# Masked attention layer with residual and norm on one core: 2304 instead of 2048 columns turned by DMA, adjacency loads split over two queues

## The chip, the cores and the metric

The kernel runs on one core of one Trainium2 chip. Its time is device time in microseconds (us). The engines of the core work side by side, each through its own list of instructions in order: TensorE (PE, with weight loads shown apart as PEld), VectorE (DVE), ScalarE (ACT), GpSimd (POOL) and SyncE (SP), which here only issues DMAs. They wait for each other by semaphores.

## The reference

```
q = x @ Wq.T + bq ; k = x @ Wk.T + bk ; v = x @ Wv.T + bv      # x is 4096 x 128, float32
scores = q @ k.T / sqrt(128)                                    # 4096 x 4096
scores = where(adj > 0, scores, -9e15)                          # adj is 4096 x 4096 int32
att = softmax(scores, axis=-1) @ v
out = layernorm(x + elu(att), axis=-1)                          # 4096 x 128
```

## The kernel before

The 4096 rows are cut in 32 tiles of 128 rows. q and k are kept in SBUF as two float16 parts each (high and low), so that three float16 matmuls give the scores of a block, and the probabilities too are split in a high and a low part before they are multiplied with v. Before the loop the projections are made; after it the last tile is finished by code of its own.

The main loop is written out as periods. Period p has eight steps j = 0 to 7 on PE, ACT and DVE, and works on several tiles at once:

- PE, in each step: the scores of 512 columns of tile p (`scores`, three matmuls); then, in the steps that `T_AT` names, the transposes of one group of 512 columns of tile p-1 or p-2 (`transposes`, four 128x128 blocks into `ps_t`); then the products with v of one group of tile p-2 in the order of `PV_ORDER` (`values`, eight matmuls).
- DVE: after every second step it adds the mask to 1024 columns of scores and takes the maximum (`masked_piece`, L589), and then turns 1024 columns of adjacency into a mask (`mask_piece`, L575). In between it makes the low parts of transposed groups (`low_part`, L604).
- ACT: the exponential of 1024 columns (`exp_piece`, L453), the high parts of transposed groups (`high_part`, L462), the high parts of rows that a DMA will turn (`high_rows`, L470), and parts of the ELU and the norm of tile p-3 (`attention` L476, `elu_exp`, `row_sum` L488, `square_sum` L492).
- POOL: the low parts of the rows that a DMA will turn (`low_rows`, L322, in pieces of 256 columns), between the small operations of ELU and norm of tile p-3 (L329 to L364).
- SP: the DMAs. `turn` transposes `p_rows[c]` (high and low halves side by side) into `p_turned[c]`; `load_half` brings half a tile of adjacency (1 MB); `store` writes a tile of output.

So a probability column reaches the product with v in one of two ways. Columns 2048 to 4095 (groups 4 to 7) are transposed on PE, copied by ACT and completed by DVE. Columns 0 to 2047 (c = 0 and c = 1) are split by ACT and POOL and transposed by DMA. The numbers at the top of the file set this:

```
DMA_COLS = (PIECE, PIECE)                  # 1024 and 1024 columns
T_AT = {4: 6, 5: 7, 6: 8, 7: 10}           # step of the transposes; 8 and 10 are 0 and 2 of the next period
PV_ORDER = (4, 5, 6, 0, 1, 7, 2, 3)        # group whose values PE takes in step 0, 1, ..., 7
```

ACT takes the high part of a group one step label after its transposes, DVE its low part likewise. The mask of a piece of scores is made three pieces ahead of its use. SP issues in a period: the turn of c = 1, the second half of the adjacency of tile p+1, the store, the turn of c = 0, and the first half of the adjacency of tile p+2.

Of the kernel before, what the change touches and what calls it, by code (L numbers as in the profile page):

```python
# [13 lines left out]
P = 128  # L14
# [15 lines left out]
LOW_PARTS = 4  # L30
# [6 lines left out]
def attention_kernel(nc, x, adj, wq, bq, wk, bk, wv, bv, out):  # L37
# [8 lines left out]
    with ExitStack() as ctx:  # L46
# [155 lines left out]
        def pv_count(i, g):  # L202

            return STEPS * i + PV_ORDER.index(g) + 1

        def exp_count(i, c):

            return PIECES * i + c + 1

# [25 lines left out]
        def _(sp):  # L235
# [44 lines left out]
            period(0, 0, head=False, turns_0=False, turns_1=False, stores=False)  # L280
# [6 lines left out]
            period(TILES - 2, 0, loads=False)  # L287
            period(TILES - 1, 1, head=False, loads=False)
# [12 lines left out]
        def _(pool):  # L301
# [14 lines left out]
            def low_rows(i, s, c):  # L316

                pool.wait_ge(rows_hi, BY_DMA * i + c + 1)
                w = DMA_COLS[c]
                for b in range(LOW_PARTS):  # L320
                    cols = slice(b * w // LOW_PARTS, (b + 1) * w // LOW_PARTS)
# [82 lines left out]
        def _(act):  # L404
# [51 lines left out]
            def high_part(i, s, g, first):  # L456
# [15 lines left out]
            def attention(i, s):  # L472

                act.wait_ge(recip_ready, i + 1)
                act.wait_ge(pv_done, STEPS * (i + 1))
# [19 lines left out]
            def last_high_part(g):  # L495

                act.wait_ge(last_pt, g - LAST_PE + 1)
                act.wait_ge(pv_done, STEPS * LAST)
                nc.scalar.activation(last_high(g), last_ps[g], ACT.Copy).then_inc(last_hi_act, 1)

            def period(p, n, has_1=True, has_2=True, has_3=True, warm=True):

                for j in range(STEPS):
                    if not warm:
# [24 lines left out]
            period(0, 0, has_1=False, has_2=False, has_3=False, warm=False)  # L529
# [3 lines left out]
            with act.Fori(2, TILES // 2) as pair:  # L533
                for n in range(2):
                    period(2 * pair + n, n)
            high_part(LAST - 1, 0, 5, False)
# [21 lines left out]
        def _(dve):  # L558
# [19 lines left out]
            def masked_piece(i, s, c, first):  # L578

                cols = slice(c * PIECE, (c + 1) * PIECE)  # L580
                if not first:
                    if c < BY_DMA:
                        dve.wait_ge(rows_lo, BY_DMA * (i - 2) + c + 1)
# [17 lines left out]
            def low_part(i, s, g):  # L601
                k = g - FIRST_PE
                dve.wait_ge(phi_ready, PE_GROUPS * i + k + 1)
                nc.vector.tensor_tensor(p_lo[:, k, :], ps_t[bank_of(s, g)][:, :], p_hi[:, k, :],  # L604
# [8 lines left out]
            def late_high_part(g):  # L613
# [3 lines left out]
                dve.wait_ge(pv_done, STEPS * (LAST - 1))  # L617
                nc.vector.tensor_copy(p_hi[:, k, :], ps_t[bank_of(0, g)][:, :]).then_inc(phi_ready, 1)

            def last_high_part(g):  # L620

                dve.wait_ge(last_pt, g - LAST_PE + 1)
                dve.wait_ge(pv_done, STEPS * (LAST - 1))
# [41 lines left out]
            def period(p, n, has_scores=True, has_1=True, has_2=True, warm=True, makes_mask=True):  # L665

                for j in range(STEPS):
# [14 lines left out]
                    if j == 1 and has_scores:  # L682
                        mask_piece(p, n, 3)
                    if j in (3, 5, 7) and has_scores and makes_mask:
                        mask_piece(p + 1, 1 - n, j // 2 - 1)


            for n in range(AHEAD):
                low_of_projection(n)
                if n > AHEAD - PIECES:  # L690
                    mask_piece(0, 0, n - AHEAD + PIECES - 1)
# [7 lines left out]
            low_part(LAST - 1, 0, 5)  # L699
# [13 lines left out]
        def _(pe):  # L713
# [70 lines left out]
            def transposes(i, s, g, first):  # L784
# [7 lines left out]
                for b in range(BLOCKS):  # L792
# [4 lines left out]
            def values(i, s, g, first):  # L797

                if g >= FIRST_PE:
                    pe.wait_ge(plo_ready, PE_GROUPS * i + g - FIRST_PE + 1)  # L800
                elif g % 2 == 0 or pv_count(0, g - 1) > pv_count(0, g):
                    pe.wait_ge(turned[g // 2], 16 * i + 16)
                if g == PV_ORDER[0] and not first:
# [5 lines left out]
                for b in range(BLOCKS):  # L809
                    k = g * BLOCKS + b  # L810
                    if g >= FIRST_PE:
                        high = p_hi[:, g - FIRST_PE, b * P:(b + 1) * P]
                        low = p_lo[:, g - FIRST_PE, b * P:(b + 1) * P]
                    else:
                        high = p_turned[g // 2][s][:, g % 2 * BLOCKS + b, :]
                        low = p_turned[g // 2][s][:, DMA_COLS[g // 2] // P + g % 2 * BLOCKS + b, :]
                    nc.tensor.matmul(ps_out[s][:, 0:2 * D], high, v_parts[:, k, :],  # L817
                                     start=(g == PV_ORDER[0] and b == 0), stop=False)
                    last = nc.tensor.matmul(ps_out[s][:, D:2 * D], low, v_parts[:, k, D:2 * D],  # L819
                                            start=False, stop=(g == PV_ORDER[-1] and b == BLOCKS - 1))  # L820
# [27 lines left out]
            def period(p, n, has_scores=True, has_1=True, has_2=True, warm=True, first=False):  # L848

                for j in range(STEPS):  # L850
# [12 lines left out]
                    if has_2:  # L863
                        values(p - 2, n, PV_ORDER[j], first)

# [11 lines left out]
            values(LAST - 1, 0, 4, False)  # L877
            values(LAST - 1, 0, 0, False)
            values(LAST - 1, 0, 1, False)
            transposes(LAST - 1, 0, 7, False)  # L880
            values(LAST - 1, 0, 5, False)
# [3 lines left out]
            for g in (7, 2, 3):  # L885
                values(LAST - 1, 0, g, False)
# [25 lines left out]
```

## Time and profile before

| | us |
|---|---|
| median of 3 runs (lowest, highest) | 434.79 (434.63, 434.86) |
| the profiled execution's own time | 434.68 |
| its span, first to last instruction | 432.8 |

| engine | busy us (share of the span) |
|---|---|
| PE | 422.2 (98%) |
| DVE | 364.2 (84%) |
| ACT | 355.2 (82%) |
| POOL | 344.5 (80%) |

The mean granted clock of TensorE is 0.996 of full speed. The queue q1, which carries all the large DMAs, has packets in flight for 92.5% of 16 engines' span; this sum counts overlapping packets twice, since it passes 1.00 in some stretches, so it is no measure of how full the DMA engines are. Ends of matmuls are modelled; their starts are what spacing is read from.

### The profile page before, as it was taken

Reading aid. Unit: us, or ns where it says so; the run is one execution under the profiler, and the core shown is the slowest. Engines: PE = TensorE matmul, PEld = TensorE weight load, DVE = VectorE, ACT = ScalarE, POOL = GpSimd, SP = SyncE. Lnnn points to the kernel's source line nnn. Section 1 sums busy time; section 2 is a strip of 40 time slices with the busy share of each in tenths; the row PEclk is TensorE's granted clock in tenths of the full one; section 3 lists DMA queues with packets and bytes.
Section 4 is the critical chain, followed back from the end, with each engine's and each line's share of the span. In section 5 each row is a group of like instructions: output and inputs, shape, how many; then the busy total and the mean of one; then the engine's idle time right before and its main releaser. Section 6 shows DMA issues by size and latency. Waiting matters only on the chain.

```text
span 432.8 us, 11401 instructions
## 1 busy us (share of the span) xinstructions
PE 422.2 (98%) x3479; PEld 310.9 (72%) x3479; DVE 364.2 (84%) x671; ACT 355.2 (82%) x737; POOL 344.5 (80%) x613
## 2 busy tenths in 40 slices
PE   8998899999999999999999999999999999999994
PEld 6564677777777777777777777777777777777783
DVE  1787998888889898888889988888898988888784
ACT  4779778888888888888888988888888988888892
POOL 0065558889888988898888988898889888898874
PEclk9999999999999999999999999999999999999998
DMA  8934999999999999999999999999999999999551
GB/s 225 380 111 121 259 271 229 258 230 267 285 268 264 266 258 278 256 271 254 261 266 270 252 254 281 272 256 245 271 266 267 251 263 274 264 252 239 103 87 36
DMA packets 149932, 104.76 MB, mean 242 GB/s; under 512 B 133024, under 2 KB 141728, under 8 KB 141728
## 3 DMA queue, kind: packets, MB, share of 16 engines
q1 hardware_dynamic: 149488, 104.41, 92.5%
q10 hardware_dynamic: 432, 0.20, 0.2%
q8 instruction: 6, 0.10, 0.1%
q14 instruction: 6, 0.05, 0.0%
HBM read 69.47 MB, written 2.10 MB: 165 GB/s over the span
## 4 chain that ended last, share of the span: by engine, by line
POOL 58%; issue 18%; PE 16%; ACT 3%; DVE 3%; POOLq 2%; ACTq 0%; DVEq 0%
POOL p_rows L322 25%; POOL res L336 6%; POOL rstd L360 4%; POOL neg_mean L347 3%; POOL y L341 3%; POOL var L356 3%; POOL att_sum L329 3%; POOL att L331 3%; PE ps_out L817 3%; POOL centred L349 2%; POOL expm L338 2%; POOL var_eps L358 2%; PE ps_scores L778 2%; PE ps_scores L779 2%; POOL y_out L364 2%
## 5 line engine op out<-in xcount | busy, mean ns | idle before, releaser
L322 POOL TENSOR_TENSOR p_rows<-scores,p_rows 128x256 f16<-128x256 f32 x252 | 176.0, 728 | 8.6 <-ACT p_rows L470 8.6
L589 DVE CUSTOM_DVE_ANT_0 scores<-ps_scores,adj 128x1024 f32<-128x1024 f32 x128 | 156.1, 1219 | 14.8 <-issue 11.3
L453 ACT ACTIVATE scores<-scores,neg_max 128x1024 f32<-128x1024 f32 x128 | 145.7, 1138 | 0.7 <-DVE neg_max L598 0.5
L575 DVE TENSOR_SCALAR adj<-adj 128x1024 f32<-128x1024 int32 x128 | 105.1, 821 | 0.0
L604 DVE TENSOR_TENSOR p_lo<-ps_t,p_hi 128x512 f16<-128x512 f32 x124 | 82.6, 685 | 26.1 <-ACT p_hi L462 25.9
L778 PE MATMUL ps_scores<-k_hi,q_hi 128*128 128x512 f16 x256 | 97.0, 379 | 0.1
L779 PE MATMUL ps_scores<-k_lo,q_hi 128*128 128x512 f16 x256 | 97.0, 379 | 0.0
L780 PE MATMUL ps_scores<-k_hi,q_lo 128*128 128x512 f16 x256 | 97.0, 379 | 0.0
L817 PE MATMUL ps_out<-v_parts,p_hi 128*128 128x256 f16 x496 | 95.3, 273 | 0.7 <-DVE p_lo L604 0.7
L817 PE MATMUL ps_out<-v_parts,p_turned 128*128 128x256 f16 x496 | 95.0, 273 | 0.0
L819 PE MATMUL ps_out<-v_parts,p_lo 128*128 128x128 f16 x496 | 88.5, 219 | 0.0
L819 PE MATMUL ps_out<-v_parts,p_turned 128*128 128x128 f16 x496 | 88.4, 219 | 0.0
L462 ACT ACTIVATE p_hi<-ps_t 128x512 f16<-128x512 f32 x122 | 71.7, 587 | 19.2 <-PE ps_t L794 18.1
L794 PEld LDWEIGHTS ps_t<-ident,scores 128*128 128x128 f32 x496 | 61.6, 141 | 25.8 <-ACT scores L453 2.6
L794 PE MATMUL ps_t<-ident,scores 128*128 128x128 f32 x496 | 74.5, 273 | 1.6 <-ACT scores L453 1.1
L470 ACT ACTIVATE p_rows<-scores 128x1024 f16<-128x1024 f32 x63 | 66.0, 1047 | 0.0
L817 PEld LDWEIGHTS ps_out<-v_parts,p_hi 128*128 128x128 f16 x496 | 48.5, 98 | 18.4 <-DVE p_lo L604 10.5
L817 PEld LDWEIGHTS ps_out<-v_parts,p_turned 128*128 128x128 f16 x496 | 48.5, 98 | 11.3
L819 PEld LDWEIGHTS ps_out<-v_parts,p_turned 128*128 128x128 f16 x496 | 48.5, 98 | 7.8
L819 PEld LDWEIGHTS ps_out<-v_parts,p_lo 128*128 128x128 f16 x496 | 48.5, 98 | 4.4
L780 PEld LDWEIGHTS ps_scores<-k_hi,q_lo 128*128 (+1 forms) x256 | 25.1, 98 | 30.2
L488 ACT ACTIVATE act_junk<-y 128x128 f32<-128x128 f32 x31 | 9.6, 310 | 37.0 <-POOL y L341 37.0
(92 smaller groups left out, 475.9 us busy)
## 6 DMA issues: line engine op xcount, KB each, us to landing
adj<-in_adj_dram SPq DMA_DIRECT2D x64, 1024.0 KB, 5.5
out_dram<-y_out SPq DMA_DIRECT2D x32, 64.0 KB, 5.1
x_rows<-in_x_dram SPq DMA_DIRECT2D x4, 256.0 KB, 4.4
x_rows<-in_x_dram SPq DMA_DIRECT2D x2, 512.0 KB, 6.6
p_turned<-p_rows SPq DMA_TRANSPOSE x63, 4.7
w_rows<-in_L_gnn_Wq_dram ACTq DMA_DIRECT2D x1, 64.0 KB, 2.7
w_rows<-in_L_gnn_Wk_dram ACTq DMA_DIRECT2D x1, 64.0 KB, 3.3
w_rows<-in_L_gnn_Wv_dram ACTq DMA_DIRECT2D x1, 64.0 KB, 3.9
```

The lines of the kernel that those rows point to most:

```text
L322: last = nc.gpsimd.tensor_tensor(p_rows[c][:, w:][:, cols], s_sb[s][:, c * PIECE:c * PIECE + w][:, cols], p_rows[c][:, 0:w][:, cols], ALU. ...
L453: nc.scalar.activation(s_sb[s][:, cols], s_sb[s][:, cols], ACT.Exp, bias=neg_max[:, s:s + 1], accum_out=p_sums[:, s, c:c + 1]).then_inc(ex ...
L462: nc.scalar.activation(p_hi[:, k, :], ps_t[bank_of(s, g)][:, :], ACT.Copy).then_inc(phi_ready, 1)
L575: nc.vector.tensor_scalar(mask_sb[s][:, cols], adj_sb[s][:, cols], 0.0, MASKED / SCALE, ALU.is_le, ALU.mult).then_inc(mask_ready, 1)
L589: nc.vector.tensor_tensor_reduce(out=s_sb[s][:, cols], in0=ps_scores[c % 2][:, :], in1=mask_sb[s][:, cols], scale=SCALE, scalar=-3.0e38, o ...
L604: nc.vector.tensor_tensor(p_lo[:, k, :], ps_t[bank_of(s, g)][:, :], p_hi[:, k, :], ALU.subtract).then_inc(plo_ready, 1)
L778: nc.tensor.matmul(place, q_hi[:, rows], k_hi[:, cols], start=True, stop=False)
L779: nc.tensor.matmul(place, q_hi[:, rows], k_lo[:, cols], start=False, stop=False)
L780: last = nc.tensor.matmul(place, q_lo[:, rows], k_hi[:, cols], start=False, stop=True)
L794: last = nc.tensor.transpose(ps_t[bank][:, b * P:(b + 1) * P], s_sb[s][:, kb * P:(kb + 1) * P], ident[:, :])
L817: nc.tensor.matmul(ps_out[s][:, 0:2 * D], high, v_parts[:, k, :], start=(g == PV_ORDER[0] and b == 0), stop=False)
L819: last = nc.tensor.matmul(ps_out[s][:, D:2 * D], low, v_parts[:, k, D:2 * D], start=False, stop=(g == PV_ORDER[-1] and b == BLOCKS - 1))
```

## The change

Columns 2048 to 2303, the first half of group 4, go the DMA's way: `p_rows[1]` and `p_turned[1]` grow from 1024 to 1280 columns. PE transposes only the two other blocks of group 4, in the same step as group 5, and group 7 one step earlier. The order of the values becomes 5, 4 (two blocks), 6, then 7 and 0 in one step, 1, 2, 3, and last the two turned blocks of group 4. Masks are made one piece ahead of their use. The first half of the adjacency of tile p+1 is issued by ACT in step 3 of period p; the second half stays on SP, behind the turn of c = 1.

```diff
-DMA_COLS = (PIECE, PIECE)
+MIXED_COLS = 256
+DMA_COLS = (PIECE, PIECE + MIXED_COLS)
+MIXED = FIRST_PE
-T_AT = {4: 6, 5: 7, 6: 8, 7: 10}
-PV_ORDER = (4, 5, 6, 0, 1, 7, 2, 3)
+T_AT = {4: 6, 5: 6, 6: 8, 7: 9}
+PV_STEPS = ((5,), (4,), (6,), (7, 0), (1,), (2,), (3,), (TURNED_HALF,))
-LOW_PARTS = 4
+LOW_COLS = 256
...
+        def by_pe(g):
+            return slice(MIXED_COLS, BANK) if g == MIXED else slice(0, BANK)
...
-            def period(p, n, head=True, turns_0=True, turns_1=True, stores=True, loads=True):
+            def period(p, n, turns_0=True, turns_1=True, stores=True, loads=True):
                 if turns_1:
                     turn(p - 2, n, 1)
-                if head:
+                if loads:
                     load_half(p + 1, 1 - n, 1, False)
                 if stores:
                     store(p - 4, n)
                 if turns_0:
                     turn(p - 1, 1 - n, 0)
-                if loads:
-                    load_half(p + 2, n, 0, False)
...
             def low_rows(i, s, c):
-                for b in range(LOW_PARTS):
+                for b in range(w // LOW_COLS):
...
             def high_part(i, s, g, first):
-                nc.scalar.activation(p_hi[:, k, :], ps_t[bank_of(s, g)][:, :], ACT.Copy).then_inc(phi_ready, 1)
+                nc.scalar.activation(p_hi[:, k, by_pe(g)], ps_t[bank_of(s, g)][:, by_pe(g)], ACT.Copy).then_inc(phi_ready, 1)
             def high_rows(i, s, c, first):
-                act.wait_ge(exp_done, exp_count(i, c))
+                act.wait_ge(exp_done, exp_count(i, (c * PIECE + w - 1) // PIECE))
...
+            def load_first_half(i, slot):
+                act.wait_ge(masked_ready, PIECES * (i - 2) + 2)
+                cols = slice(0, 2 * PIECE)
+                act.dma_start(adj_sb[slot][:, cols], adj_tiled[i, :, cols]).then_inc(adj_in[slot][0], 16)
+
                 for j in range(STEPS):
+                    if j == 3 and loads:
+                        load_first_half(p + 1, 1 - n)
...
-                    if j == 1 and has_scores:
-                        mask_piece(p, n, 3)
-                    if j in (3, 5, 7) and has_scores and makes_mask:
-                        mask_piece(p + 1, 1 - n, j // 2 - 1)
+                    if j in (1, 3, 5) and has_scores:
+                        mask_piece(p, n, j // 2 + 1)
+                    if j == 7 and has_scores and makes_mask:
+                        mask_piece(p + 1, 1 - n, 0)
```

On PE, in steps 1 to 3 of a period of the loop, the order before is as follows (`p_turned_0` is a buffer of `p_turned[0]`; matmuls of the same kind follow each other where a pair is shown).

```order
L778 MATMUL ps_scores<-k_hi,q_hi 128x512
L779 MATMUL ps_scores<-k_lo,q_hi 128x512
L780 MATMUL ps_scores<-k_hi,q_lo 128x512
L794 MATMUL ps_t<-ident,scores 128x128 x4
L800 REGISTER_ALU
L817 MATMUL ps_out<-v_parts,p_hi 128x256
L819 MATMUL ps_out<-v_parts,p_lo 128x128
```

These are the rows of step 2: scores, the transposes of group 7, the values of group 6. The changed kernel has in steps 1 and 3:

```order
L808 MATMUL ps_t<-ident,scores 128x128 x4
L836 MATMUL ps_out<-v_parts,p_hi 128x256
L838 MATMUL ps_out<-v_parts,p_lo 128x128
L836 MATMUL ps_out<-v_parts,p_hi 128x256
L838 MATMUL ps_out<-v_parts,p_lo 128x128
L792 MATMUL ps_scores<-k_hi,q_hi 128x512
```
```order
L836 MATMUL ps_out<-v_parts,p_hi 128x256
L838 MATMUL ps_out<-v_parts,p_lo 128x128
L819 ISA
L836 MATMUL ps_out<-v_parts,p_turned_0 128x256
L838 MATMUL ps_out<-v_parts,p_turned_0 128x128
```

The first piece is step 1: the transposes of group 7 now stand there, before two blocks of values of group 4. The second is step 3: the last values from `p_hi` and `p_lo` (group 7) stand ahead of the first turned ones (group 0); before, group 7 stood two steps later.

On DVE, from the start of a period, before:

```order
L604 TENSOR_TENSOR p_lo<-ps_t,p_hi 128x512
L603 REGISTER_ALU
L604 TENSOR_TENSOR p_lo<-ps_t,p_hi 128x512
L583 ISA
L586 ISA
L589 ISA scores,max_parts<-ps_scores,adj 128x1024
L589 ISA max_parts 128x1
L608 ISA
L609 TENSOR_REDUCE p_sum<-p_sums 128x1
L611 RECIPROCAL recip<-p_sum 128x1
L574 ISA
L575 TENSOR_SCALAR adj<-adj 128x1024
```

and after:

```order
L619 TENSOR_TENSOR p_lo<-ps_t,p_hi 128x512
L598 ISA
L601 ISA
L604 ISA scores,max_parts<-ps_scores,adj 128x1024
L604 ISA max_parts 128x1
L623 ISA
L624 TENSOR_REDUCE p_sum<-p_sums 128x1
L626 RECIPROCAL recip<-p_sum 128x1
L589 ISA
L590 TENSOR_SCALAR adj<-adj 128x1024
L618 REGISTER_ALU
L619 TENSOR_TENSOR p_lo<-ps_t,p_hi 128x512
```

One of the two low parts at the head has gone to the period before. The low part of group 7 stands, before and after, behind the first masked piece, the reciprocal and the mask.

On ACT, from the copy of the attention output to the next exponential, before:

```order
L476 ACTIVATE att<-ps_out,recip 128x256
L467 ISA
L469 REGISTER_ALU
L470 ACTIVATE p_rows<-scores 128x1024
L459 REGISTER_ALU
L461 REGISTER_ALU
L462 ACTIVATE p_hi<-ps_t 128x512
L453 ACTIVATE scores,p_sums<-scores,neg_max 128x1024
```

and after:

```order
L482 ACTIVATE att<-ps_out,recip 128x256
L465 REGISTER_ALU
L467 REGISTER_ALU
L468 ACTIVATE p_hi<-ps_t 128x512
L473 ISA
L475 REGISTER_ALU
L476 ACTIVATE p_rows<-scores 128x1024
L509 REGISTER_ALU
L511 ISA
L511 DMA adj<-in_adj_dram 128x2048
L459 ACTIVATE scores,p_sums<-scores,neg_max 128x1024
```

The high part of group 7 has moved ahead of the rows for the DMA, and the load stands behind them.

## Rows read from the trace of the kernel before

**Rows 1.** Stretch: us; busy PE, PEld, DVE, ACT, POOL; PEclk, DMA share, GB/s.
```profile
200.00:250.00 50.00, 50.00 (x428) 37.08 (x427) 44.08 (x81) 41.70 (x88) 43.94 (x79) 1.00 0.99 264
```
**Rows 2.** Timeline of PE: start us, us, instruction, count.
```profile
204.06 0.38 PE L778 MATMUL ps_scores<-k_hi,q_hi 128*128 128x512 f16 x1
...
204.71 0.60 PE L794 MATMUL ps_t<-ident,scores 128*128 128x128 f32 x4
...
205.15 0.27 PE L817 MATMUL ps_out<-v_parts,p_hi 128*128 128x256 f16 x1
...
205.81 0.38 PE L778 MATMUL ps_scores<-k_hi,q_hi 128*128 128x512 f16 x1
...
206.24 0.38 PE L780 MATMUL ps_scores<-k_hi,q_lo 128*128 128x512 f16 x1
...
208.90 0.38 PE L778 MATMUL ps_scores<-k_hi,q_hi 128*128 128x512 f16 x1
...
209.55 0.27 PE L817 MATMUL ps_out<-v_parts,p_turned 128*128 128x256 f16 x1
```
**Rows 3.** Timeline of DVE, same stretch.
```profile
205.76 1.27 DVE L604 TENSOR_TENSOR p_lo<-ps_t,p_hi 128x512 f16<-128x512 f32 x2
206.95 1.21 DVE L589 CUSTOM_DVE_ANT_0 scores<-ps_scores,adj 128x1024 f32<-128x1024 f32 x1
...
208.35 0.78 DVE L575 TENSOR_SCALAR adj<-adj 128x1024 f32<-128x1024 int32 x1
209.15 0.69 DVE L604 TENSOR_TENSOR p_lo<-ps_t,p_hi 128x512 f16<-128x512 f32 x1
...
211.04 1.06 DVE L575 TENSOR_SCALAR adj<-adj 128x1024 f32<-128x1024 int32 x1
```
**Rows 4.** Timeline of POOL over one period.
```profile
202.57 2.57 POOL L322 TENSOR_TENSOR p_rows<-scores,p_rows 128x256 f16<-128x256 f32 x4
...
208.54 3.01 POOL L322 TENSOR_TENSOR p_rows<-scores,p_rows 128x256 f16<-128x256 f32 x4
211.52 0.90 POOL L336 TENSOR_TENSOR res<-pos,x_rows 128x128 f32<-128x128 f32 x1
...
214.82 2.57 POOL L322 TENSOR_TENSOR p_rows<-scores,p_rows 128x256 f16<-128x256 f32 x4
```
**Rows 5.** What POOL's L329 waited for, 100 to 390 us: us, times.
```profile
  ACT att L476: 9.5, 23
```
**Rows 6.** Timeline of ACT.
```profile
201.13 0.31 ACT L488 ACTIVATE act_junk<-y 128x128 f32<-128x128 f32 x1 [1.26 <-POOL y L341]
...
201.44 1.04 ACT L470 ACTIVATE p_rows<-scores 128x1024 f16<-128x1024 f32 x1
```
**Rows 7.** POOL in the last periods, where DVE makes no masks.
```profile
407.17 0.45 POOL L336 TENSOR_TENSOR res<-pos,x_rows 128x128 f32<-128x128 f32 x1
...
415.58 2.56 POOL L322 TENSOR_TENSOR p_rows<-scores,p_rows 128x256 f16<-128x256 f32 x4
```
**Rows 8.** Timeline of SP's DMA issues.
```profile
70.69 2.76 SPq L263 DMA_TRANSPOSE p_turned<-p_rows  x1
...
205.24 3.00 SPq L263 DMA_TRANSPOSE p_turned<-p_rows  x1
208.48 0.39 SPq L249 DMA_DIRECT2D adj<-in_adj_dram  x1
...
388.66 3.12 SPq L263 DMA_TRANSPOSE p_turned<-p_rows  x1
```
**Rows 9.** DMA by issue: KB each, median us from issue to landing.
```profile
adj<-in_adj_dram SPq DMA_DIRECT2D x64, 1024.0 KB, 5.5
...
p_turned<-p_rows SPq DMA_TRANSPOSE x63, 4.7
```
**Rows 10.** Stretches with loads alone (first) and a turn alone, columns as rows 1.
```profile
14.00:19.00 5.00, 5.00 (x21) 2.29 (x20) 3.84 (x6) 3.65 (x7) 0.00 (x0) 1.00 1.01 426
...
421.50:422.50 1.00, 1.00 (x15) 0.93 (x13) 0.75 (x2) 1.00 (x5) 0.84 (x4) 1.00 1.27 290
```

More of the change, by code:

```diff
@@ L286, in _ @@
                     period(2 * pair + n, n)
-            period(TILES - 2, 0, loads=False)
-            period(TILES - 1, 1, head=False, loads=False)
+            period(TILES - 2, 0)
+            period(TILES - 1, 1, loads=False)
             turn(LAST - 1, 0, 1)
@@ L527, in period @@
                         square_sum(p - 3, 1 - n, pool_done, POOL_OPS * (p - 3))
-            period(0, 0, has_1=False, has_2=False, has_3=False, warm=False)
+            period(0, 0, has_1=False, has_2=False, has_3=False, warm=False, loads=False)
             period(1, 1, has_2=False, has_3=False, warm=False)
@@ L532, in _ @@
             period(3, 1)
-            with act.Fori(2, TILES // 2) as pair:
+            with act.Fori(2, TILES // 2 - 1) as pair:
                 for n in range(2):
                     period(2 * pair + n, n)
-            high_part(LAST - 1, 0, 5, False)
+            period(LAST - 1, 0)
+            period(LAST, 1, loads=False)
             exp_piece(LAST, 1, 0, False)
@@ L581, in masked_piece @@
                 if not first:
[L582 to L583 removed]
+                    if 2 * c <= MIXED:
+                        dve.wait_ge(rows_lo, BY_DMA * (i - 2) + min(c + 1, BY_DMA))
                     if 2 * c + 1 >= FIRST_PE:
@@ L791, in transposes @@
                     pe.wait_ge(plo_ready, PE_GROUPS * i + k - 1)
-                for b in range(BLOCKS):
+                for b in range(by_pe(g).start // P, BLOCKS):
                     kb = g * BLOCKS + b
@@ L795, in transposes, with values @@
                 last.then_inc(pt_ready, 1)
-            def values(i, s, g, first):
-                if g >= FIRST_PE:
+            def values(i, s, part, first):
+                g = MIXED if part == TURNED_HALF else part
+                by_dma = part < FIRST_PE or part == TURNED_HALF
+                c = min(g // 2, BY_DMA - 1)
+                if not by_dma:
                     pe.wait_ge(plo_ready, PE_GROUPS * i + g - FIRST_PE + 1)
-                elif g % 2 == 0 or pv_count(0, g - 1) > pv_count(0, g):
-                    pe.wait_ge(turned[g // 2], 16 * i + 16)
-                if g == PV_ORDER[0] and not first:
+                elif part % 2 == 0:
+                    pe.wait_ge(turned[c], 16 * i + 16)
+                if part == PV_ORDER[0] and not first:
                     pe.wait_ge(att_ready, i - 1)
@@ L862, in period @@
                             transposes(p - 1, 1 - n, g, not warm)
-                    if has_2:
-                        values(p - 2, n, PV_ORDER[j], first)
+                    for g in PV_STEPS[j]:
+                        if has_2:
+                            values(p - 2, n, g, first)
             period(0, 0, has_1=False, has_2=False, warm=False)
@@ L876, in _ @@
             transposes(LAST - 1, 0, 6, False)
-            values(LAST - 1, 0, 4, False)
-            values(LAST - 1, 0, 0, False)
-            values(LAST - 1, 0, 1, False)
+            for part in (5, 4, 0, 1):
+                values(LAST - 1, 0, part, False)
             transposes(LAST - 1, 0, 7, False)
-            values(LAST - 1, 0, 5, False)
             values(LAST - 1, 0, 6, False)
@@ L884, in _ @@
             last_transposes(3)
-            for g in (7, 2, 3):
-                values(LAST - 1, 0, g, False)
+            for part in (7, 2, 3, TURNED_HALF):
+                values(LAST - 1, 0, part, False)
             for g in range(FIRST_PE, STEPS):
```

41 lines of the change are left out of this document (22 added, 19 removed).

## The prediction

> **What bounds the kernel now.** I read the table of stretches first. In the middle of the run PE is busy for 50.00 us of 50, at full clock, while POOL has 43.94, DVE 44.08 and ACT 41.70 [rows 1]. So PE sets the pace of the loop, and the reader should ask at once how far behind it the others are. The pace itself: the turn of c = 1 is issued at 70.69, 205.24 and 388.66 us, which is 12.23 us per tile over 26 periods [rows 8]. With the two or three periods on either side of these I count 29 that run at this pace.
>
> Then the timelines, engine by engine over one period. On PE a step takes 0.65 us for its scores (208.90 to 209.55), 0.44 for four transposes (204.71 to 205.15) and 0.66 for eight matmuls of values (205.15 to 205.81) [rows 2]. Eight steps and four sets of transposes make 8 x 1.31 + 4 x 0.44 = 12.24, so PE has next to no waits in its 12.23.
>
> POOL comes second, and closer than its 88% says. Its waits are mostly answers that it has to wait for whatever the pace. The one that shows slack is L329's wait for ACT's copy of the attention output, 9.5 us in 23 periods, 0.41 us each [rows 5]. If PE went faster or POOL had more to do, that 0.41 is what it could give.
>
> The DMA side looks full at 0.99 [rows 1], but it is not. Loads alone move 426 GB/s, a turn alone 290, and the share reads 1.27 there [rows 10]. Two loads of 1.05 MB at 426 are 4.9 us and two turns of 0.52 MB at 290 are 3.6 us, together 8.5 of 12.23.
>
> **The change, part by part.**
>
> PE's work. Per tile two transposes of 128 columns go: 2 x 0.11 = 0.22 us. Number and kind of the scores and values stay. PE alone would then need 12.23 - 0.22 = 12.01 us per tile. Over 29 periods this is the gain on offer, 6.4 us.
>
> PE's new wait, the first term that decides. The values of group 7 move from step 5 to step 3. They need DVE's low part of group 7, and DVE makes that behind the first masked piece, the reciprocal and a mask, before as after. I count from the start of step 0, at 204.06. PE now begins step 1 at 1.75, as before; step 2 at 1.75 + 0.65 + 0.44 + 0.33 (half a set of values) = 3.17; step 3 at 3.17 + 0.65 + 0.66 = 4.48; it wants the values of group 7 at 4.48 + 0.65 = 5.13 [rows 2]. DVE starts the first masked piece at 206.95, which is 2.89, the mask at 4.29, the low part at 5.09, and ends it at 209.84, which is 5.78 [rows 3]. DVE was busy with two low parts until 207.03, of which one is now earlier; but the masked piece also needs the third scores matmul of step 1, which starts at 206.24 and lasts 0.38 [rows 2], so it can come forward by at most about 0.15 us. The low part ends at 5.63 to 5.78, and PE waits 0.50 to 0.65 us. Behind it stand the values of group 0, the scores of step 4 and all else on PE; nothing on PE makes the time up. PE's loop becomes 12.01 + 0.58 = 12.59 us.
>
> POOL's work, the second term. `low_rows` of c = 1 gets a fifth piece: 2.57 / 4 = 0.64 us, or 3.01 / 4 = 0.75 where DVE's masks lie across it [rows 4]. ACT's `high_rows` of c = 1 grows from 1024 to 1280 columns, 1.04 x 256 / 1024 = 0.26 us by proportion. This lies on POOL's path too: POOL makes y, ACT sums it (start 201.13), makes the high rows (201.44 to 202.48), and POOL starts the low rows at 202.57 [rows 4, 6]. Against these stands the 0.41 of slack. POOL's loop is 12.23 - 0.41 + 0.64 + 0.26 = 12.72 us. What is uncertain is how DVE's masks lie on POOL. `res` takes 0.90 us and four low pieces 3.01 with masks, 0.45 and 2.56 at the end, where DVE makes none [rows 4, 7]: a mask costs POOL up to 0.45 us when POOL has work under it. If one of the four masks falls in an idle stretch, the loop is 12.27; with the dearer piece and no relief it is 12.83.
>
> On this point the Trainium skill (SBUF — State Buffer, section "SBUF: two separate sides") says that VectorE in a two-port mode and GpSimd share one pair of ports under an exclusive lock, and that the one that starts first keeps it for the whole instruction. The doubled `res` agrees, and so does the mask of 1.06 us at 211.04, beside 0.78 at 208.35 [rows 3]. By that rule a POOL piece begun just before the mask of step 1 would hold that mask too; this is the third rival below.
>
> The other edits, at nothing. The high part of group 4 shrinks by half, and that of group 7 moves ahead of the high rows of c = 0 on ACT; ACT has idle time of 1.26 us per tile in front of L488, where it waits for POOL's y [rows 6], and this hides the 0.39 us too that the load's issue would cost it if it costs ACT what it costs SP [rows 8]. If that cover went, it would be 0.39 per tile at most. The masks keep their number and their places in DVE's list; only which piece is made changes. The turn of c = 1 has 2560 packets' worth instead of 2048: its 3.00 us of issue become about 3.75 and its landing goes from 4.7 to about 5.5 [rows 8, 9]; its first reader is PE in step 5 and ACT's next high rows, 8 us after the issue. Below nothing, the changed order could save a little in the first tiles, since two masks are no longer made ahead of the loop; I give it nothing.
>
> The load of the first half is issued by ACT behind the high rows of c = 0, at about 209, and needed by the mask of step 7, which stood at 205.12 + 12.23 = 217.35 in this frame. It lands 5.5 us after its issue if alone [rows 9], at 214.5. But SP issues the second half at the same time (208.48, plus 0.75 for the longer turn) [rows 8]. Both at 426 GB/s need 4.9 us instead of 2.5, so it lands at about 217. That is just in time, and I count nothing.
>
> **The sum.** The loop takes the slower of PE's 12.59 and POOL's 12.72. The new idle of POOL in front of the low rows gives a mask a place to fall for free, so I take a little off the second: 12.65 us. That is 0.42 more than 12.23, times 29 = 12.2 us. The profiled execution took 434.68 us (its span 432.8 and 1.9 around it); 434.68 + 12.2 = 446.9. The median of the runs lies 0.11 above the profiled one, so I predict 447.0 us. Its own range is 441 to 453, a loop of 12.45 to 12.85.
>
> **The rivals.**
>
> A. PE goes on setting the pace, faster than before. The point that decides is when DVE ends the low part of group 7: at 5.13 us PE waits for nothing, the loop is 12.01 and the time 434.8 - 6.4 = 428.4. To break even it must come at 5.35, 0.3 or more ahead of my 5.63. POOL must also keep within 12.23, which asks that more than one mask stops holding it. For this speaks that the trace shows one phase only between DVE and POOL, and four masks could cost POOL little in another; against it, that DVE's chain from the scores of step 1 is made of durations alone, without a wait in it. Chance 0.06.
>
> B. The two loops come out near the old one: one mask free of POOL (12.27), and a wait on PE of 0.2 to 0.3. Then the time is 434 to 436. Chance 0.03.
>
> C. The mask of step 1 is held by a POOL piece: 1.06 instead of 0.78, 0.28 more on PE's wait, a loop of 12.9. That is 29 x 0.67 = 19.4 more, 454. For it speaks that POOL will now be late against PE, so that its pieces lie elsewhere; against it, that in the trace small operations of 0.46 us stand there. Chance 0.09.
>
> D. The first half of the adjacency comes late. Each 0.5 us that the mask of step 7 waits for beyond its time delays the masked piece of the next step 1, and with it the low part of group 7: 12.65 + 0.5, which is 29 x 0.92 = 27 more, 461. For it speaks that two loads and soon a turn share the engines; against it, that a longer period also moves the mask of step 7 later by 0.4. Chance 0.10.
>
> E. My forecast, 0.72.
>
> About 0.2% is what a measurement of this kernel can tell from no change. Faster: 0.06, same: 0.03, slower: 0.91. The range for 8 in 10 goes from 438, a loop of 12.34, near POOL's lower bound, to 457, which takes in C and the mild half of D.
>
> **What would show it.** In the profile after: PE's busy time below its span in the loop, with its longest wait in front of the values of `p_hi` for DVE's p_lo, near 0.6 us per tile, in step 3. POOL's wait of L329 for ACT gone to nearly nothing, and a new one in front of its fifth-piece group for ACT's p_rows. Five low pieces in the second group. ACT's wait for y longer than 1.26. The turn of c = 1 spaced at 12.65. No wait of DVE for adj; were there one, D holds. My forecast is wrong if the turns come at 12.23 or less, or if PE shows no wait in step 3.

## The result, and the profile after

| | before | after |
|---|---|---|
| median (lowest, highest), us | 434.82 (434.63, 434.86) | 462.37 (458.29, 464.78) |
| ratio, 95% interval | | 1.0624 [1.0583, 1.0665] |
| profiled execution: time; span | 434.68; 432.8 | 464.78; 463.0 |
| first copy of the attention output starts | 60.24 | 67.58 |
| spacing of these copies, mean over 24 periods (4th to 28th) | 12.228 | 12.986 |
| from the 28th copy to the end of the span | 42.4 | 45.0 |

The changed kernel is 6.2% slower, where 447.0 with a range to 457 was forecast: the direction holds, the time lies outside the range. Ratios are of fast runs alone, within 1.5% of the fastest of the same kernel, which leaves out two of e4's four. The profiled execution is the slowest of the four; the sums below are made against its own span. The 30.2 us of it come from three places: 7.3 before the first copy, 20.2 in the 27 periods up to the 28th, and 2.7 at the end. The forecast had only the second, at 12.2.

The page, engines first, then the stretch that answers to [rows 1]:

```profile
PE 423.7 (92%) x3417; PEld 301.3 (65%) x3417; DVE 349.7 (76%) x671; ACT 358.6 (77%) x737; POOL 346.0 (75%) x644
```
```profile
200.00:250.00 50.00, 47.37 (x397) 34.19 (x398) 39.56 (x76) 40.30 (x87) 41.98 (x79) 1.00 0.93 260
```

PE, busy without a gap before, now has 2.6 us of idle in 50, at full clock, and no engine took its place: every one is less busy than before. A loop of waits sets the pace. The spacing itself, by ACT's copies:

```profile
197.53 0.46 ACT L482 ACTIVATE att<-ps_out,recip 128x256 f32<-128x256 f32 x1
...
210.16 0.46 ACT L482 ACTIVATE att<-ps_out,recip 128x256 f32<-128x256 f32 x1
...
223.36 0.46 ACT L482 ACTIVATE att<-ps_out,recip 128x256 f32<-128x256 f32 x1
...
235.99 0.47 ACT L482 ACTIVATE att<-ps_out,recip 128x256 f32<-128x256 f32 x1
```

12.63, 13.20, 12.63: the short periods have the length forecast (12.65), and every second one is longer, mostly by 0.5 to 0.75. PE's timeline of the long one shows two waits (for [rows 2]; before, the first row of values stood 0.22 after the start of the third scores matmul):

```profile
212.05 0.38 PE L794 MATMUL ps_scores<-k_hi,q_lo 128*128 128x512 f16 x1
212.90 0.28 PE L836 MATMUL ps_out<-v_parts,p_hi 128*128 128x256 f16 x1 [0.47 <-DVE p_lo L619]
...
215.97 0.38 PE L794 MATMUL ps_scores<-k_hi,q_lo 128*128 128x512 f16 x1
216.76 0.28 PE L836 MATMUL ps_out<-v_parts,p_turned 128*128 128x256 f16 x1 [0.41 <-DMA p_turned<-p_rows]
```

The first is step 3 and group 7: 212.90 - 212.05 - 0.22 = 0.63 us, the wait that was forecast. The second is step 5 and group 2, the first reader of the turn of c = 1: 0.57 us, and it was forecast to be free. What PE's weight loads waited for, in total (us, times, longest), over the whole span; the matmuls behind them waited 15.5 and 13.0 us, and of the second sum one wait of 5.7 is that of the start:

```profile
PEld ps_out L836 <- DVE p_lo L619: 30.5, 31, 1.7
...
PEld ps_out L836 <- DMA p_turned<-p_rows: 20.7, 16, 6.2
```

The turn that PE waits for there, on SP and in the DMA, with the load that ACT issues beside it (for [rows 8, 9]):

```profile
208.87 3.04 SPq L272 DMA_TRANSPOSE p_turned<-p_rows  x1
```
```profile
210.67 0.34 ACTq L511 DMA_DIRECT2D adj<-in_adj_dram  x1
```
```profile
L272 SPq DMA_TRANSPOSE p_turned<-p_rows x1: 3041/3041/3041, 208.9 to 208.9; - x1
...
DMA to landing us min/median/max: 7.8/7.8/7.8
```

208.87 + 7.8 is 216.67, and PE starts at 216.76. In the short period that follows, the turn is issued at 221.51 and lands in 7.5, and its first reader starts at 229.39, 7.9 behind the issue, without a wait. The turn of c = 0 one half period before the late one, with no load of ACT's near its issue, lands in 5.9. Over the turns issued between 80 and 390 us, those of c = 1 land in 7.7 (median; 6.4 to 8.1) and those of c = 0 in 6.4 (5.9 to 7.4); before it was 4.7 and 4.6.

The late landing has a mark of its own. SP ends the issue of the turn of c = 1 after 3.0 us, as quickly as before, and the landing comes 4.6 us behind that end (median; 3.4 to 5.0). For the turns of c = 0 it comes 2.0 behind it, and before the change 1.7 for both.

POOL, for [rows 4] (c = 1 first, then c = 0 and `res`), and ACT's wait for y, for [rows 6]:

```profile
205.49 3.28 POOL L328 TENSOR_TENSOR p_rows<-scores,p_rows 128x256 f16<-128x256 f32 x5 [0.49 <-ACT p_rows L476]
...
212.13 3.01 POOL L328 TENSOR_TENSOR p_rows<-scores,p_rows 128x256 f16<-128x256 f32 x4 [0.43 <-ACT p_rows L476]
215.10 0.45 POOL L342 TENSOR_TENSOR res<-pos,x_rows 128x128 f32<-128x128 f32 x1
```
```profile
216.47 0.31 ACT L494 ACTIVATE act_junk<-y 128x128 f32<-128x128 f32 x1 [1.42 <-POOL y L347]
```

The fifth piece costs 3.28 - 2.57 = 0.71. `res` takes 0.45 instead of 0.90: one of DVE's masks no longer lies across it, as the forecast had allowed for.

The late start is one event. ACT and POOL, whose first high and low rows of 1280 columns wait:

```profile
59.64 1.27 ACT L476 ACTIVATE p_rows<-scores 128x1280 f16<-128x1280 f32 x1 [8.89 <-DMA p_turned<-p_rows]
```
```profile
60.99 3.18 POOL L328 TENSOR_TENSOR p_rows<-scores,p_rows 128x256 f16<-128x256 f32 x5 [9.41 <-ACT p_rows L476]
```

They wait for a turn that SP issued at 46.25; ACT issued its first load 0.8 us behind it, SP the second half at 48.67, and the turn landed after 13.3 us:

```profile
46.25 2.37 SPq L272 DMA_TRANSPOSE p_turned<-p_rows  x1
48.67 1.08 SPq L258 DMA_DIRECT2D adj<-in_adj_dram  x1
```
```profile
47.04 0.33 ACTq L511 DMA_DIRECT2D adj<-in_adj_dram  x1
```
```profile
L272 SPq DMA_TRANSPOSE p_turned<-p_rows x1: 2369/2369/2369, 46.2 to 46.2; - x1
...
DMA to landing us min/median/max: 13.3/13.3/13.3
```

The next turn, of c = 0, starts its issue at 51.67, and that takes 10.2 us. Meanwhile the engines are idle and the DMA's share is as high as ever, while it moves a fraction of the 290 to 426 GB/s of [rows 10]:

```profile
55.00:56.00 1.00, 0.00 (x0) 0.00 (x0) 0.90 (x3) 0.00 (x0) 0.00 (x0) 1.00 1.35 84
56.00:57.00 1.00, 0.00 (x0) 0.00 (x0) 0.00 (x0) 0.00 (x0) 0.00 (x0) 1.00 1.30 57
57.00:58.00 1.00, 0.00 (x0) 0.00 (x0) 0.00 (x0) 0.00 (x0) 0.00 (x0) 1.00 1.21 36
```

### The profile page after: what moved, and what is told of

It is laid out like the page before. It is cut to its first block, busy times and chain, and to the rows that moved or that the text cites. A ratio compares the mean times of both kernels' runs of the same rounds, so it can differ in the third digit from the quotient of the medians.

```text
span 463.0 us, 11266 instructions
## 1 busy us (share of the span) xinstructions
PE 423.7 (92%) x3417; PEld 301.3 (65%) x3417; DVE 349.7 (76%) x671; ACT 358.6 (77%) x737; POOL 346.0 (75%) x644
## 4 chain that ended last, share of the span: by engine, by line
POOL 52%; DMA 13%; ACT 11%; issue 11%; PE 11%; POOLq 1%; DVE 1%; ACTq 0%; SPq 0%; DVEq 0%
POOL p_rows L328 32%; DMA p_turned<-p_rows 12%; ACT p_rows L476 8%; POOL rstd L366 4%; POOL y L347 3%; POOL att L337 2%; POOL res L342 2%; POOL att_sum L335 2%; PE ps_t L732 2%; POOL expm L344 2%; PE ps_out L743 2%; POOL var L362 1%; POOL y_out L370 1%; POOL var_eps L364 1%; ACT act_junk L494 1%
## 5 line engine op out<-in xcount | busy, mean ns | idle before, releaser
L328 POOL TENSOR_TENSOR p_rows<-scores,p_rows 128x256 f16<-128x256 f32 x283 | 198.2, 731 | 43.4 <-ACT p_rows L476 43.4
L836 PE MATMUL ps_out<-v_parts,p_turned 128*128 128x256 f16 x558 | 109.2, 274 | 13.0 <-DMA p_turned<-p_rows 13.0
L838 PE MATMUL ps_out<-v_parts,p_turned 128*128 128x128 f16 x558 | 100.8, 220 | 0.0
L836 PE MATMUL ps_out<-v_parts,p_hi 128*128 128x256 f16 x434 | 85.2, 273 | 15.5 <-DVE p_lo L619 15.5
L619 DVE TENSOR_TENSOR p_lo<-ps_t,p_hi 128x256 f16<-128x256 f32 (+1 forms) x124 | 76.6, 619 | 24.7 <-ACT p_hi L468 23.9
L468 ACT ACTIVATE p_hi<-ps_t 128x256 f16<-128x256 f32 (+1 forms) x122 | 66.0, 542 | 29.5 <-PE ps_t L808 27.9
L476 ACT ACTIVATE p_rows<-scores 128x1024 f16<-128x1024 f32 (+1 forms) x63 | 73.1, 1160 | 9.9 <-DMA p_turned<-p_rows 9.5
L838 PE MATMUL ps_out<-v_parts,p_lo 128*128 128x128 f16 x434 | 78.3, 219 | 0.0
L836 PEld LDWEIGHTS ps_out<-v_parts,p_turned 128*128 128x128 f16 x558 | 54.7, 98 | 34.6 <-DMA p_turned<-p_rows 20.7
L836 PEld LDWEIGHTS ps_out<-v_parts,p_hi 128*128 128x128 f16 x434 | 42.4, 98 | 37.5 <-DVE p_lo L619 30.5
L808 PE MATMUL ps_t<-ident,scores 128*128 128x128 f32 x434 | 63.0, 274 | 2.3 <-ACT scores L459 2.3
L838 PEld LDWEIGHTS ps_out<-v_parts,p_turned 128*128 128x128 f16 x558 | 54.8, 98 | 9.1
```

The lines of the kernel that those rows point to most:

```text
L476: nc.scalar.activation(p_rows[c][:, 0:w], s_sb[s][:, c * PIECE:c * PIECE + w], ACT.Copy).then_inc(rows_hi, 1)
L619: nc.vector.tensor_tensor(p_lo[:, k, by_pe(g)], ps_t[bank_of(s, g)][:, by_pe(g)], p_hi[:, k, by_pe(g)], ALU.subtract).then_inc(plo_ready, 1)
L808: last = nc.tensor.transpose(ps_t[bank][:, b * P:(b + 1) * P], s_sb[s][:, kb * P:(kb + 1) * P], ident[:, :])
```

## The experiments

Each ran beside the kernel before on the same chip. "After" in a kernel's description is the changed kernel. "Spacing" is the mean of the 24 periods as in the table above, "start" the first copy of the attention output; before has 12.228 and 60.24.

| kernel | median us (range) | ratio [95%] | spacing | start |
|---|---|---|---|---|
| e1 columns part alone | 447.14 (446.97–447.82) | 1.0278 [1.0260, 1.0295] | 12.618 | 60.44 |
| e2 loads and masks part alone | 434.89 (434.52–435.61) | 0.9998 [0.9988, 1.0007] | 12.238 | 59.95 |
| e3 after, POOL four pieces | 448.34 | 1.0298 [1.0281, 1.0315] | 12.628 | 61.41 |
| e4 after, group 7 in step 5 | 462.9, of 461.04 and 464.81; of all four 466.91 (461.04–469.48) | 1.0635 [1.0584, 1.0686] | 13.082 | 66.86 |
| e5 e1, group 7 in step 5 | 446.36 (445.27–447.32) | 1.0257 [1.0239, 1.0276] | 12.603 | 59.47 |
| e6 e5, POOL four pieces | 440.98 (438.34–443.72) | 1.0150 [1.0092, 1.0208] | 12.377 | 59.40 |
| e7 after, ACT's load in step 5 | 450.56 (448.19–453.15) | 1.0344 [1.0305, 1.0384] | 12.620 | 66.54 |
| e9 e5, fifth piece on DVE | 441.50 (440.42–443.67) | 1.0146 [1.0126, 1.0166] | 12.366 | 59.37 |
| e12 e1, old order | 445.41 (445.18–445.81) | 1.0243 [1.0226, 1.0260] | 12.585 | 59.79 |
| e10 e12, fifth piece on DVE | 443.88 (442.33–444.30) | 1.0209 [1.0192, 1.0226] | 12.497 | 60.31 |
| e11 after, first three loads on SP | 457.42 (456.96–457.90) | 1.0514 [1.0496, 1.0531] | 13.011 | 59.95 |
| e13 e12 with 128 columns | 435.87 (435.20–437.19) | 1.0027 [1.0015, 1.0038] | 12.260 | 60.19 |

**The two halves of the change.** e1 keeps the 2304 columns and the new order, with loads and masks as before:

```diff
+                if loads:
+                    load_half(p + 2, n, 0, False)
...
-                    if j == 3 and loads:
-                        load_first_half(p + 1, 1 - n)
...
-                    if j in (1, 3, 5) and has_scores:
-                        mask_piece(p, n, j // 2 + 1)
+                    if j == 1 and has_scores:
+                        mask_piece(p, n, 3)
...
```

> The 2304 columns, the new order of transposes and values, but both loads on SP's queue at their old places and the masks three pieces ahead as before. Theory 1 (the loop is set by POOL and ACT, and the load on ACT's queue costs about 8 us once in the first tiles plus some turns that come late): the 8 us go and the loop loses its long odd periods, about 13.0 to 12.65 us per tile, so 443 to 448 us. Rival 1 (the longer turn itself is what comes late, whichever queue the loads are on): no more than 3 us below the changed kernel, 457 to 462. Rival 2 (PE's wait for the low part of group 7 sets the loop): 12.5 us per tile and 442 us.

e2 is the reverse, the kernel before with ACT's load and the later masks:

```diff
...
+                    if j == 3 and loads:
+                        load_first_half(p + 1, 1 - n)
...
```

> The kernel before, with 2048 columns by DMA and its own order on PE, but the loads split over the two queues and the masks one piece ahead as in the changed kernel. Theory 1: the first tiles cost about 8 us more, and in the loop PE still sets the pace at 12.23 us, so 441 to 444 us. Rival 1 (only the longer turn is at fault): 435 us, no change. A third view (a load beside a turn delays every turn enough to stall PE in every period): over 450 us.

e1 takes 447.14, the forecast time, and its start is on time. e2 takes nothing. So the columns cost 12.4 us, the loads by themselves 0, and together there are 15 more: an interaction. In e1 SP queues the second half of the adjacency right behind the longer turn, and in the middle of the run the turn lands in 5.3:

```profile
L272 SPq DMA_TRANSPOSE p_turned<-p_rows x1: 3570/3570/3570, 204.9 to 204.9; - x1
...
DMA to landing us min/median/max: 5.3/5.3/5.3
```

Over all turns of c = 1 from 80 to 390 us the median in e1 is 5.0. But the range goes from 4.8 to 7.3: in e1's first periods SP issues each turn about 1 us behind a load, and the issue itself is held up.

```profile
96.63 0.35 SPq L258 DMA_DIRECT2D adj<-in_adj_dram  x1
97.47 5.16 SPq L272 DMA_TRANSPOSE p_turned<-p_rows  x1
```

This turn lands in 7.2, still only 2.0 us behind the end of its issue. So one queue alone can make a turn late too, by a load ahead of it. What one queue never shows in the loop of e1 is a quick issue and a late landing: there the landing comes 1.5 us behind the end of the issue in the median and 2.1 at most, in the changed kernel 4.6.

In e2 ACT's load is issued at 207.38, when SP has just ended the issue of the turn of c = 1 (205.12 to 207.05), and the turn lands in 4.4. The turns of c = 0 land in 5.9 there, where they landed in 4.6 before, and nobody waits for them.

**The two terms of the sum.** e3 drops POOL's fifth piece from the changed kernel; the low parts of columns 2048 to 2303 are zeros, set once. e4 puts group 7 in step 5.

```diff
-                for b in range(w // LOW_COLS):
+                for b in range(min(4, w // LOW_COLS)):
```

> The changed kernel without POOL's fifth piece: the low parts of columns 2048 to 2303 are left out (that part of p_rows holds zeros, set once before the loop), all else the same. Theory 1 (POOL's loop): 0.64 us less per tile on POOL, so the loop falls until PE with its wait for group 7 takes over at about 12.5: 13.0 to 12.5, some 14 us below the changed kernel, 446 to 450 us. Rival 2 (PE's wait sets the loop): no change, 458 to 465. Rival 3 (late turns set it): no change either.

```diff
-PV_STEPS = ((5,), (4,), (6,), (7, 0), (1,), (2,), (3,), (TURNED_HALF,))
+PV_STEPS = ((5,), (4,), (6,), (0,), (1,), (7, 2), (3,), (TURNED_HALF,))
```

> The changed kernel with the values of group 7 taken in step 5 as before the change, ahead of those of group 2, instead of in step 3. Theory 1: PE's wait of about 0.45 us in step 3 goes, but POOL's loop stays, so no more than 3 us less, 458 to 463 us. Rival 2 (PE's wait for group 7 sets the loop): 0.45 x 29 = 13 us less, about 449 us.

e3 saves 14 us. Its turns of c = 1 land as late as ever (median 7.5), but POOL's work was on their path: they are now issued earlier relative to PE, and the weight loads wait for `p_turned` 1.1 us in four times between 100 and 390 us. What stays is PE's loop alone, 12.628. e4 saves nothing: PE, without its wait in step 3, runs into the turned columns, for which its weight loads wait 35.3 us in 20 times over the span (its profile, and with it its spacing, is of an execution of 469.01 us). With that in the way e4 says nothing of PE's term, so e5 repeats e4's diff on e1, where from 100 to 390 us no matmul waits for a turn, and e6 repeats e3's diff on top of e5.

> The columns-only version (loads and masks as before the change) with the values of group 7 back in step 5. Theory 1 (two loops of nearly the same length stand behind 12.6 us per tile: PE's through the low part of group 7, and POOL's): PE's wait in step 3 goes, POOL's loop stays, so 0 to 4 us below the columns-only version, 443 to 447. Rival 2 (PE's wait alone sets it): 12.1 us per tile, 14 us less, 433 us.

> The same, and POOL's fifth piece left out too (the low parts of columns 2048 to 2303 hold zeros). Theory 1: neither loop is left, PE's own work of about 12.0 us per tile sets the pace, 428 to 431 us, faster than the kernel before. Rival 4 (the longer turn or ACT's wider high rows hold the loop as well): 435 us or more.

e5 has only POOL's loop and runs at 12.603; e3 has only PE's and runs at 12.628; e1 has both and runs at 12.618. They are two loops of one length, and taking either away gives nothing. POOL's wait for the attention output bears this out: between 100 and 390 us it comes 22 times in e3 (15.1 us), once in e5 and never in e1. In e5 the transposes of step 0 now wait for ACT's exponential, the sign of a late ACT behind POOL's y, for which ACT waits up to 1.77 us there:

```profile
210.55 0.65 PE L803 MATMUL ps_t<-ident,scores 128*128 128x128 f32 x4 [0.44 <-ACT scores L462]
```

e6 takes both away and misses its forecast: 12.377 instead of about 12.0. POOL is down to four pieces and 39.5 us of 50. In this stretch SP's turns and loads stand back to back, with about 5 us of issue for each turn, and PE waits for one turn that lands in 7.7, though no load is on ACT's queue:

```profile
201.67 4.59 SPq L272 DMA_TRANSPOSE p_turned<-p_rows  x1
206.56 0.34 SPq L258 DMA_DIRECT2D adj<-in_adj_dram  x1
207.14 5.68 SPq L272 DMA_TRANSPOSE p_turned<-p_rows  x1
213.06 0.38 SPq L258 DMA_DIRECT2D adj<-in_adj_dram  x1
```
```profile
214.89 0.28 PE L832 MATMUL ps_out<-v_parts,p_turned 128*128 128x256 f16 x1 [0.51 <-DMA p_turned<-p_rows]
```

The prediction had the DMA 70% full (8.5 of 12.23 us), by bytes and rates. That leaves out what the issues take: here the two turns alone hold SP for 10.3 us of a period, and each stands close behind a load. This stretch is not all of e6, though. The median of its 24 periods is 12.31, and eight longer ones, up to 12.68, make the mean of 12.377.

**The same with real work.** e9 is e5 with the fifth low piece made by DVE in step 7, behind the row maximum; e12 is e1 with the old transposes and value order (the turned half of group 4 after group 3), e10 is e12 with the fifth piece on DVE.

```diff
+                    if j == 7 and has_1:
+                        mixed_low(p - 1, 1 - n)
```

> The columns-only version with group 7 in step 5, and the fifth low piece made by DVE at the end of the period instead of by POOL, so that all is computed. Theory 1: POOL's loop is 0.64 us shorter, DVE has the room (some 2 us idle per tile), PE sets the pace at 12.0 to 12.1 us: 428 to 433 us, below the kernel before. Rival 6 (DVE's later low parts stall PE instead): 435 to 442 us.

```diff
-T_AT = {4: 6, 5: 6, 6: 8, 7: 9}
+T_AT = {4: 6, 5: 7, 6: 8, 7: 10}
-PV_STEPS = ((5,), (4,), (6,), (7, 0), (1,), (2,), (3,), (TURNED_HALF,))
+PV_STEPS = ((4,), (5,), (6,), (0,), (1,), (7,), (2,), (3, TURNED_HALF))
```

> The columns part alone with the old order of transposes and value products, POOL making five low pieces. Theory 1 (POOL's loop of 12.6 alone is enough): 440 to 446 us. Rival 2 (only PE's wait in step 3 holds the period): 428 to 432.

> Columns part alone (both halves of the load on SP's queue), with the fifth low piece made by DVE instead of POOL, and the old order of the transposes and the product with the values (so that PE's wait in step 3 for p_lo of group 7 is as before). Theory 1 (the two loops of about 12.6 us are the fifth POOL piece and PE's wait in step 3): 428 to 431 us. Rival 7 (a third loop, ACT's third exp behind two high parts, or the full queue of the turn, holds the period at 12.3 to 12.4): 436 to 441.

e12 has no new wait in step 3, and still 12.585, and between 100 and 390 us POOL never waits for the attention output: its slack is gone, as the POOL term says. How the delay gets to PE is less clean. PE waits 0.62 us in step 1 for DVE's low part of group 5 (210.92 - 210.08 - 0.22), which stands behind a mask of 1.04 us; whether that wait alone would hold the loop as well, no run separates.

e9 and e10 miss. e9 runs at 12.37 in nearly every period, with all work done. Its one gap on PE beyond the usual spacing is in front of the transposes of step 0, which wait for ACT's exponential:

```profile
210.64 0.65 PE L812 MATMUL ps_t<-ident,scores 128*128 128x128 f32 x4 [0.18 <-ACT scores L462]
```

They start 0.57 after the third scores matmul (210.07) instead of 0.22 after it. That is 0.35 on top of PE's 12.01, which makes 12.36. The settled periods of e6 have the same gap, 0.48 (306.19 - 305.71), which makes 12.27 for a measured 12.31. So there is a third loop, at 12.3 to 12.4, through ACT's exponential. e10 alternates between 12.1 and 12.9; in its long periods PE waits for DVE in step 1:

```profile
222.46 0.28 PE L842 MATMUL ps_out<-v_parts,p_hi 128*128 128x256 f16 x1 [0.74 <-DVE p_lo L615]
```

**The interaction.** e7 moves ACT's load from step 3 to step 5, behind the issue of the turn of c = 1. e11 lets SP issue both halves in periods 1 to 3, behind the turn, and ACT from period 4 on.

```diff
-                    if j == 3 and loads:
+                    if j == 5 and loads:
```

> The changed kernel with ACT's load issued in step 5 instead of step 3, some 3 us later, so that the turn of c = 1 has its data moved before the load starts. Theory 1 (the load on the second queue shares the DMA engines with the end of that turn, and PE waits for it): the turn of c = 1 lands in about 5 us instead of 7.7, the waits of PE for it go, and the loop is at 12.6: 447 to 451 us. Rival 5 (any load on a second queue slows whichever turn is there): 455 us or more, with the turn of c = 0 late instead.

```diff
+                if both:
+                    load_half(p + 1, 1 - n, 0, False)
...
-            period(1, 1, turns_1=False, stores=False)
+            period(1, 1, turns_1=False, stores=False, both=True)
```

> The changed kernel, with both halves of the loads of the first periods (1 to 3) issued on SP's queue, and the first half on ACT's queue only from period 4 on. Theory 1 (the first att comes 7 us late because a turn is in flight beside the other queue's load there): first att at about 60 instead of 67.6 us, time 455 to 458. Rival 8 (the late start has another cause): 460 to 464.

e7 brings the loop back to 12.62, and moves the delay to the other turn. That of c = 0 (issued at 211.10; ACT's load at 209.36, ahead of it) now takes 5.6 us to issue and lands in 7.8, and nobody waits for it; that of c = 1 lands in 4.8:

```profile
L272 SPq DMA_TRANSPOSE p_turned<-p_rows x1: 5578/5578/5578, 211.1 to 211.1; - x1
...
DMA to landing us min/median/max: 7.8/7.8/7.8
```
```profile
L272 SPq DMA_TRANSPOSE p_turned<-p_rows x1: 3122/3122/3122, 217.3 to 217.3; - x1
...
DMA to landing us min/median/max: 4.8/4.8/4.8
```

Over 80 to 390 us the turns of c = 1 land in 4.8 to 4.9, all 24 of them. Its start is nearly as late as the changed kernel's (66.54 against 67.58): there ACT's load, at 47.23, still falls 0.3 us behind the start of the turn's issue, at 46.94. e11 is the complement: start at 59.95, loop at 13.011 with the waits for the turn still there (15.0 us in 18 times on the weight loads between 100 and 400 us). Its turn issued at 47.07, the one that took 13.3 us, lands in 4.8, and ACT's high rows wait 0.99 instead of 8.89:

```profile
52.00 1.27 ACT L478 ACTIVATE p_rows<-scores 128x1280 f16<-128x1280 f32 x1 [0.99 <-DMA p_turned<-p_rows]
```

The spans say the same: 463.0 to 456.1 for e11. The medians differ by 5.0, since the changed kernel's runs scatter over 6.5 us.

**Half as many columns.** e13 turns 128 more columns by DMA, in the old order, the fifth piece half as wide.

```diff
-MIXED_COLS = 256
+MIXED_COLS = 128
```

> Only 128 columns more than before are turned by DMA. Theory 1 (half a piece of POOL work fits into the slack of about 0.4 us that POOL has in the kernel before): 432 to 436 us. Rival (PE's saved transposes come out in full): 431.5 or less.

435.87, a trifle slower than before: half a piece nearly fits into POOL's 0.41 of slack, of which nothing is left (POOL no longer waits for the attention output), and PE's saved transpose (0.11 a tile) doesn't come out. No version tried beats the kernel before.

## Why the prediction was wrong

**PE's new wait: right.** 0.50 to 0.65 us forecast in step 3; 0.63 measured there in the changed kernel, and PE's loop alone is 12.628 in e3 (forecast 12.59). The masked piece of step 1 started at 209.99 and the low part of group 7 at 212.16, which is 2.84 and 5.01 after the start of step 0 (207.15): the chain of durations held, with no wait in it.

**POOL's fifth piece: right in size.** 0.64 to 0.75 forecast, 0.71 measured; the loop 12.65 forecast, 12.603 and 12.585 measured in e5 and e12. POOL's slack is gone as forecast: it still waits for the attention output (0.33 or 0.70 us) only in the long periods. The relief of one mask was real. The Trainium skill (SBUF — State Buffer, "SBUF: two separate sides") has VectorE in a two-port mode and GpSimd exclude each other on a shared port pair. `res` at 0.45 with no mask across it and 0.90 with one agrees. Rival C, the held mask, did not come: the mask of step 1 took 0.80.

**ACT's edits: half right.** The issue of the load cost ACT 0.34 us and was hidden. But POOL now waits for ACT at both of its groups (0.49 and 0.43), not at the fifth-piece group alone. The high part of group 7, now ahead of the high rows of c = 0, can't be the whole cause: e1 has it there too, and POOL waits for ACT at one group a period only (24 times between 100 and 390 us, against 45 in the changed kernel).

**"The other edits, at nothing": the step that failed.** The sentence was that the turn's landing "goes from 4.7 to about 5.5; its first reader is PE in step 5 ... 8 us after the issue". In the long period shown PE wanted it 7.3 us after the issue (216.19 - 208.87), and it took 7.8; the median over the loop is 7.7, not 5.5. The prediction had seen that two loads would share the DMA engines and asked only when the loads would land. It never asked what a load on a second queue does to the turn in flight beside it. POOL's fifth piece has its part, since it is what makes the issue of that turn late: without it (e3) the turn lands in 7.5 and costs next to nothing.

Four kernels separate this. With ACT's load issued while SP is still issuing the turn of c = 1, that turn lands late (the changed kernel, 7.7). With the load issued two steps later and nothing else changed (e7), it lands in 4.9, and it is the turn of c = 0 that is late. With the loads on SP's queue (e1) the median is 5.0. With the short turn, already issued when the load comes, the load is harmless (e2). The Trainium skill (DMA: Bandwidth & Descriptors, "Queues, rings and completion order") has each DMA engine alternate between the queues that have work, a packet at a time; by it SP's turn loses time to ACT's load, and a load behind it in the same queue takes none. The runs agree, with 4.6 us from the end of the issue to the landing in the changed kernel against 1.5 in e1; that packets are what alternates, no run here shows. Nor is the second queue the only way to a late turn: in e6, with all loads on SP's, the turns of c = 1 land in 7.1 (median), each behind a load on the same queue.

The price in the loop: 27 periods at 12.98 (350.4 / 27) against e1's 12.62 (340.9 / 27), 9.5 us. e1, without ACT's load, takes 447.14, so the forecast of 447.0 was good for the columns part; for the whole change it lacks this term and the next.

**The start: a term that was missing.** I had given the first tiles "nothing". A collision of the same two queues, in the periods where the engines wait for each tile in turn, cost 7.3 us once, against e1 7.1; e11 takes it away alone. The mark is the same: the turn issued at 46.25 is issued in 2.4 us and lands 10.9 behind that. It is the same two queues, but e11 also changes which DMA is issued when, so that the issue order by itself had a share is not excluded.

**Rival D** had a time of 461, but by the adjacency being late. In the profile of the changed kernel DVE never waits for `adj`; the nearness of its number is chance.

**Rival A**, PE faster at 12.01, would need more than the loss of both loops. e6 and e9, without either, stay at 12.31 and 12.37 in their settled periods. The third loop shows as PE's wait in step 0 for ACT's exponential, in front of which ACT makes two high parts (0.85 us together in e9). In e10, where only one stands there, PE has no such wait and the short periods take 12.1; but e10 changes the whole order with it, so that the high part is the cause is likely and not shown. Why e10 alternates is open too. Its DVE makes the fifth piece (0.73 us, at 220.47) just ahead of the mask and the low parts that PE waits for.

## What to carry to other kernels

When an edit moves a DMA to another queue, price what it does to the transfer already in flight, by that transfer's first reader, and not only when the moved one lands. Before a wait is costed as the new bound, list all loops within 0.4 us of the old one: here there were three between 12.3 and 12.63, and removing either of the upper two alone gained nothing. When a turn is late, look whether its issue was long (something stood ahead of it) or short (something came in beside it). And look at the first tiles apart: a clash hidden in the loop cost 7 us in them.

## What the runs showed of the hardware

- A transposing DMA of 0.66 MB (1280 high and 1280 low columns of 128 rows, float16) lands in 4.8 to 5.3 us with a 1 MB load behind it on the same queue and nothing close ahead (e7, e1). It lands in 7.7 (median; 6.4 to 8.1) when such a load comes from the other queue while it is being issued, and in 7.1 (median; 5.9 to 7.7) when loads stand close ahead of it on its own queue (e6). In the start, with 1 MB on each queue, it took 13.3, at a DMA rate that fell to 36 GB/s.
- Issuing it holds SP for 3.0 to 3.1 us (changed kernel, e7) and for 4.3 to 5.7 when a load stands close ahead (e6); a turn of 0.52 MB took 5.6 (e7) to 10.2 us (start). A long issue tells that the DMA is occupied, which the share (1.35 at 84 GB/s) doesn't. A short one tells nothing of the landing: 3.0 us of issue went with a landing at 4.9 (e7) and at 7.7 (changed kernel).
- A GpSimd operation of 0.45 us under a VectorE mask takes 0.90, and the 0.45 comes back when the phase between the two shifts.
